# Scan layer: another order of its work on all four engines

## What is computed

```python
h = x @ fc1_w.T + fc1_b
xc, z = split(h @ in_proj_w.T)                     # 512 channels each
u = silu(causal_conv4(xc) + conv_b)
dt_low, Bm, Cm = split(u @ x_proj_w.T)             # 16, 16, 16
dt = softplus(dt_low @ dt_proj_w.T + dt_proj_b)
hstate = exp(dt * A) * hstate + (dt * u) * Bm      # per channel, 16 states, along 2048 steps
y = ((hstate * Cm).sum(states) + u * D) * silu(z)
s = (y @ out_proj_w.T) @ fc2_w.T + fc2_b
f = (silu(x @ w_gate.T) * (x @ w_up.T)) @ w_down.T # 768 hidden
```

## Time and profile before

| what | value |
|---|---|
| median of 3 runs | 2787.99 us (2785.57 to 2789.45) |
| profiled execution: its own time / span | 2788.2 us / 2786.4 us |
| first layer | up to about 859 us of the span |
| scan layer | about 859 to 2786 us |
| PE, DVE, ACT, POOL busy over the span | 91%, 84%, 72%, 72% |

### The profile page before, as it was taken

How to read it: one execution, slowest core, us unless ns; L and a number is a source line. 1 busy time by engine, 2 the same in 40 slices (tenths; PEclk the granted TensorE clock), 3 DMA queues, 4 the chain that set the end, 5 groups by cost and what they waited for, 6 DMA issues and landing times. The chain is left out here.

```text
span 2786.4 us, 37406 instructions
## 1 busy us (share of the span) xinstructions
PE 2542.0 (91%) x13454; PEld 1490.8 (54%) x13454; DVE 2333.8 (84%) x2899; ACT 2011.2 (72%) x3253; POOL 2013.2 (72%) x682
## 2 busy tenths in 40 slices
PE   7897899999976799999999999999999999999988
PEld 3454344443443465656656566565655656556565
DVE  7685777777733899898998989989899898998996
ACT  4222466666643798897988979889798897988974
POOL 0656011111211999999999999999999999999996
PEclk9898999999978799999999999999999999999999
DMA  6337999888541231321313213132131321313210
GB/s 188 116 116 179 260 218 236 205 200 224 211 161 49 105 130 29 117 92 46 130 26 119 92 46 130 25 120 92 46 130 24 121 92 46 130 24 114 92 46 8
DMA packets 121586, 316.00 MB, mean 113 GB/s; under 512 B 15517, under 2 KB 76445, under 8 KB 104878
## 3 DMA queue, kind: packets, MB, share of 16 engines
q1 hardware_dynamic: 91210, 233.32, 27.3%
q0 software_dynamic: 27888, 79.24, 10.3%
q10 hardware_dynamic: 2304, 1.05, 0.2%
HBM read 278.89 MB, written 43.13 MB: 116 GB/s over the span
## 5 line engine op out<-in xcount | busy, mean ns | idle before, releaser
L1523 DVE TENSOR_TENSOR_SCAN l_st<-l_p_a,l_hl,l_st 128x512 f32<-128x512 f32 x768 | 930.2, 1263 | 90.5 <-ACT l_p_a L1808 83.3
L1721 POOL TENSOR_TENSOR l_st<-l_st,lw_cs 128x2048 f32<-128x2048 f32 x192 | 878.4, 4634 | 3.2 <-ACT l_hl L1813 3.2
L1808 ACT ACTIVATE l_p_a<-l_dt,lw_a_neg 128x512 f32<-128x512 f32 x1024 | 666.5, 681 | 67.2 <-DVE keep_xg L1523 41.1
L1713 POOL TENSOR_TENSOR l_st<-l_bs,l_dtu 128x2048 f32<-128x2048 f32 (+1 forms) x128 | 555.1, 4337 | 57.2 <-PE l_p_y L2098 53.3
L2098 PEld LDWEIGHTS l_p_y<-keep_ident,l_st 128*128 128x128 f32 x3072 | 355.1, 145 | 118.6 <-issue 73.0
L2098 PE MATMUL l_p_y<-keep_ident,l_st 128*128 128x128 f32 x3072 | 380.5, 281 | 28.7 <-POOL l_st L1721 28.7
L1020 ACT ACTIVATE a_pr<-a_p_s 128x512 f32<-128x512 f32 x512 | 284.7, 596 | 143.8 <-PE a_p_s L1089 140.0
L931 DVE TENSOR_REDUCE a_mpart<-a_p_m 128x1 f32<-128x512 f32 x512 | 312.0, 679 | 12.2 <-PE a_p_m L1045 11.0
L1523 DVE TENSOR_TENSOR_SCAN keep_xg<-l_p_a,l_hl,keep_xg 128x512 f32<-128x512 f32 x256 | 314.5, 1265 | 1.6
L1721 POOL TENSOR_TENSOR keep_xg<-keep_xg,lw_cs 128x2048 f32<-128x2048 f32 x64 | 299.7, 4682 | 2.0 <-ACT l_hl L1813 2.0
L858 POOL DMA_DIRECT2D a_w<-in_w_dram x32 | 23.1, 737 | 327.2 <-PE a_p_m L1119 271.3
(11 more groups left out here) (246 smaller groups left out, 4007.9 us busy)
## 6 DMA issues: line engine op xcount, KB each, us to landing
l_bs<-s_bc SPq DMA_DIRECT2D x64, 1024.0 KB, 4.7
lw_cs<-s_bc SPq DMA_DIRECT2D x64, 1024.0 KB, 4.7
a_w<-in_w_dram POOLq DMA_DIRECT2D x32, 1024.0 KB, 12.0
late<-in_w_dram POOLq DMA_DIRECT2D x32, 1024.0 KB, 19.4
kx<-s_kp SPq DMA_DIRECT2D x96, 256.0 KB, 12.3
s_kp<-late SPq DMA_DIRECT2D x96, 128.0 KB, 2.1
s_vp<-late SPq DMA_DIRECT2D x16, 544.0 KB, 3.5
a_vg<-s_vp SPq DMA_DIRECT2D x16, 544.0 KB, 14.8
```

The costliest lines, as they stand in the source:

```text
L1523: eng.tensor_tensor_scan(st[k % NG][:, n, :], p_a[:, n, :], st[k % NG][:, n, :], hl[:, k, n:n + 1], ALU.mult, ALU.add).then_inc(scan_ok, 1)
L1713: eng.tensor_tensor(st[n][:, first:NG, :], bs[:, 4 * n + first:4 * n + 4, :], dtu[(k // NG) % 2][:, :].unsqueeze(1).broadcast_to([P, NG - ...
L1721: eng.tensor_tensor(st[n][:, :, :], st[n][:, :, :], cs[:, 4 * n:4 * n + 4, :], ALU.mult).then_inc(cm_ok, 1)
L1808: eng.activation(p_a[:, n, :], dt[c % 2][:, :], ACT.Exp, scale=a_neg[:, c, m:m + 1]).then_inc(dA_ok, 1)
```

## The change

It edits the scan layer alone. No product, no size and no instruction of the arithmetic is changed; the order on all four engines is, and so is the bank of many fills. The last up blocks (4 and 5), dt of block 1, the first half of the down product and the sums of slots 14 and 15 move on PE from the period after into the tile's own SCAN period. The transposition of the next tile's normed rows (`turn` 0) moves to the end of the period before it. DVE's input of slot 0 and `hidden(3)` move ahead of the last scan of the previous tile, and ACT's `normed` of the next tile and the fourth exponential of slot 0 move to the end of the period before.

```diff
+        FILLS = (("tr", 1, FRONT, 1), ("dn", 1, END, 0), ("yb", 3, END, 1), ("xc", 0, FRONT, 0), ("op", 0, END, 1),
+                 ("xc", 1, FRONT, 0), ("z", 0, SCAN, 1), ("dt", 2, SCAN, 0), ("z", 1, SCAN, 0), ("op", 1, END, 1),
+                 ("cv", 0, FRONT, 0), ("dt", 3, SCAN, 1), ("xc", 2, FRONT, 0), ("cv", 1, FRONT, 1), ("cv", 2, FRONT, 0),
+                 ("yb", 0, SCAN, 1), ("xc", 3, FRONT, 1), ("g", 0, SCAN, 0), ("g", 1, SCAN, 1), ("up", 0, SCAN, 1),
+                 ("cv", 3, FRONT, 0), ("up", 1, SCAN, 1), ("xd", 0, FRONT, 0), ("g", 2, SCAN, 1), ("yb", 1, SCAN, 0),
+                 ("z", 2, SCAN, 1), ("g", 3, SCAN, 0), ("up", 2, SCAN, 0), ("yb", 2, SCAN, 1), ("dt", 0, FRONT, 1),
+                 ("g", 4, SCAN, 0), ("z", 3, SCAN, 0), ("g", 5, SCAN, 1), ("up", 3, SCAN, 0), ("up", 4, SCAN, 1),
+                 ("up", 5, SCAN, 0), ("dt", 1, FRONT, 1), ("dn", 0, SCAN, 0), ("tr", 0, NEXT, 0))
...
 # DVE, first tile's convolution: waits for the last reader of its own bank
-                    wait(eng, done["cv"], c - 1)
+                    wait(eng, done["cv"], max([x + 1 for x in range(c) if bank("cv", x) == bank("cv", c)], default=0))
...
 # DVE, end of its period
+                    if front:
+                        step_size(q, 0)
+                    if scan:
                         scan_unit(s, 14, 3)
                         scan_unit(s, 15, 0)
-                        gated(s, o, 2)
                         scan_unit(s, 15, 1)
                         scan_unit(s, 15, 2)
+                    if front:
+                        dbu(q, 0)
+                    if scan:
+                        hidden(s, 3)
                         scan_unit(s, 15, 3)
...
 # POOL
                     if end:
+                        weighed(f, 11)
+                        weighed(f, 12)
                         dbu(f, 15)
+                        weighed(f, 13)
                     if scan:
                         step_input(s, o, 0)
...
                     if scan:
+                        weighed(s, 0)
                         step_input(s, o, 1)
-                        weighed(s, 0)
                         dbu(s, 3)
                         weighed(s, 1)
                         weighed(s, 2)
                         dbu(s, 5)
                         weighed(s, 3)
-                        step_input(s, o, 2)
-                    if end and f < NT - 1:
-                        residual(f)
-                    if scan:
                         weighed(s, 4)
                         dbu(s, 7)
                         weighed(s, 5)
+                        step_input(s, o, 2)
+                    if end:
+                        residual(f)
+                    if scan:
+                        dbu(s, 9)
                         weighed(s, 6)
-                        dbu(s, 9)
                         weighed(s, 7)
...
 # ACT, end of its period
+                        exp_unit(s, 15, 2)
                     if front:
                         step_input(q, 0)
                     if scan:
-                        exp_unit(s, 15, 2)
-                        exp_unit(s, 15, 3)
+                        gate_z(s, 3)
+                        gate_h(s, 5)
+                    if nxt:
+                        normed(q + 1)
+                    if scan:
+                        exp_tables()
+                        exp_unit(s, 15, 3)
                     if front:
                         exp_unit(q, 0, 0)
                         exp_unit(q, 0, 1)
-                    if scan:
-                        gate_z(s, 3)
-                    if front:
-                        exp_tables()
                         exp_unit(q, 0, 2)
+                        exp_unit(q, 0, 3)
```

More of the change, by code:

```diff
@@ L2050, in period @@
                         exp_unit(s, 14, 3)
+                        last(s, 13)
+                    if front:
+                        step_log(q, 0)
+                    if q == 0:
+                        norm_scale(1)
+                    if scan:
                         gate_h(s, 4)
[L2052 to L2055 removed]
                         exp_tables()
@@ L2228, in period @@
                     if end:
+                        back(q, f, p, 3)
+                    if front:
+                        conv_in(q, q, p, 0)
+                    if scan:
+                        sums(s, 1)
+                    if end:
                         mix(q, f, p, 0)
+                    if front:
+                        conv_in(q, q, p, 1)
                     if scan:
+                        gate_z(q, s, o, 0)
                         step_low(q, s, 2)
-                        sums(s, 1)
                         sums(s, 2)
+                        gate_z(q, s, o, 1)
+                        sums(s, 3)
                     if end:
```

336 lines of the change are left out of this document (144 added, 192 removed).

## The result

The changed kernel takes 2779.76 us (median; 2775.17 to 2782.18) where the kernel before takes 2786.89: a ratio of 0.9973, 95% interval 0.9963 to 0.9983. It is faster by 7.1 us; some 32 were forecast (2788.2 to 2756). The profiled execution took 2782.18 us, the slowest of the nine (span 2780.4; before 2788.2, span 2786.4).

What follows compares the result with a forecast made beforehand. POOL, 112.2 us busy plus 4.0 waiting per period, was taken as the bound. Gains of 25.5 (14 periods), 1.0 (last period), 2.0 (head) and 4.0 (end), 32.5 us, took 2788.2 to about 2756 us; range 2726 to 2797.

Steps and rivals of the forecast that it cites:

- likeliest case: The forecast of 2756 us with its inner bounds, 2740 to 2776 us, given a chance of 0.54.
- Rival (b): PE's sums 5, 7, 9, 11 each a us late: period 116.1 to 116.4, total 2780 to 2790 us; chance 0.13.
- the period: Steady scan-layer period: falls from 116.2 to 114.4 us, 1.8 each, 25.5 us over 14 periods.
- the end: After POOL's last product: dn0 done before it, 5.2 us gained, about 1.1 given back, 4 us net.
- signs of being wrong: Listed refutations: POOL wait over 1.5 us; slot 15's state-3 exponential over 9 us after `step_input` 0; DVE never idle at seam.
- the last period: Last scan period, without next tile and so without seam: shorter, 1.0 us gained.
- Predicted waits: POOL's waits, in us, before `weighed` 15, `weighed` 0, `dbu` 9, `dbu` 11 and `dbu` 13; added to 112.2 giving 114.55.
- more time in the middle: A longer seam gives PE more time mid-period, so 114.4 us was taken rather than the summed 114.55.
- Head: Start of the scan layer, first tile: `weighed` 0 about 2 us earlier, bounds 2 lost to 3 gained.
- Seam and tables: Tile's seam, from S (start of POOL's `step_input` 0): last exponential done at S + 8.4; added table loads cost ACT 2.6 us.
- (c): ACT's queue at the seam late: at 3.4 us late, 117.8 us a period, 2803 us; chance 0.21 with similar chains.
- (d): Table switch holds ACT another 1.28 us: 118.2 us a period, 2809 us; chance 0.02.

Runs made afterwards that it cites:

- e1: Changed kernel with ACT saving slot 4's ends straight behind the dt logarithm of block 2, ahead of three exponentials: 2776.86 us, 0.9966.
- e13: As e12_best, with dt product 1 of the next tile ahead of the sums of slot 14 on PE: 2769.2 us, 0.993.
- e16: As e13, with the edit of e1 added: 2764.82 us, 0.9912.
- e4_si0: Changed kernel with POOL's `step_input` 0 of the next tile ahead of `weighed` 13, as before the change: 2785.99 us, 0.9997.
- e9_seam: Changed kernel with the exponential of slot 15, state 3, ahead of ACT's copy, and up block 5 ahead of S14 on PE: 2774.55 us, 0.9945.
- e7_warm: Changed kernel with constant matrix products in the last scan period; at the end yb3 ahead of dn1, second output half in the other bank: 2774.24 us, 0.9946.
- e12_best: Edits of e9_seam and e7_warm, plus last tile's last scan ahead of `hidden` 3 and first tile's `conv_in` 3 ahead of `conv_out` 2: 2769.83 us, 0.9929.
- e3_tail: Changed kernel with op0 ahead of S1 in the last scan period; at the end yb3 ahead of dn1, second output half in the other bank: 2778.76 us, 0.9971.
- e17_dt2: As e13, with dt product 2 and the sums of slot 2 ahead of z0 on PE: 2774.06 us, 0.9948.
- e5_s9: Changed kernel with PE's sums of slot 9 ahead of the xd product instead of behind it: 2790.94 us, 1.0002.
- e10_undo_s1: Changed kernel with op0 ahead of S1 on PE again: 2797.91 us, 1.0034.
- e11_undo_s9: Changed kernel with g2 ahead of S9 on PE again: 2853.7 us, 1.0227.
- e2_exp15: Changed kernel with ACT's exponential of slot 15, state 3, ahead of the copy of dt*u, z3, g5 and the next tile's norm: 2773.78 us, 0.9957.
- e6_s7s9: Changed kernel with PE's S9 ahead of the xd product and S7 ahead of g1: 2796.57 us, 1.0031.

## Why the prediction was wrong

The direction was right, the amount was not: 32.5 us of gains were added up, 6.0 came in this execution. The median, 2779.76 us, lies in the wide range and outside the likeliest case, 2740 to 2776. Rival (b) all but names the time (2780 to 2790) but not the cause, since the period did shorten and the end was lost. One of the prediction's own signs of being wrong came: POOL waits over 1.5 us, 3.43 in the first period and 2.38, 1.51 and 1.57 in the last. Two steps failed by their mechanism and had the wrong sign, the last period and the end, 14.1 of the 26.5 us that are missing; the period, 8.1, was mis-sized.

**The period: mechanism right, size off.** Predicted waits 0.65, 0.4, 0.15, 0.65 and 0.5; measured 0.66, 0.34, 0, 0.35 and 0.53. One was missed: 0.70 before `weighed` 4, whose `last` now stands behind a logarithm and three exponentials. POOL's 112.3 and these five waits, 2.6, make the 114.9; the plain sum was 114.55. The further 0.15 for "more time in the middle" had no row and did not come. Over 14 periods 17.4 us instead of 25.5: 8.1 short, some 4.6 by the sum, 2.1 by the 0.15, and 1.4 because the gain of 1.8 was taken from 116.2, while the 14 periods were 116.12 each. The counting was of POOL's waits, which tells what a given order costs; what one of them is worth it does not tell (e1, e13, e16).

**The last period, 1.0 us forecast, 6.75 lost.** This step failed first. It was written down as one more, shorter period in one clause, with no walk. By the prediction's own rule, that only POOL's waits can be won, nothing could be gained: the kernel before has none there. Putting S1 ahead of op0 is right where PE has the front's blocks; without them PE idles 3.1 us ahead of S1, and in this execution its clock fell there, through a stretch in which POOL now hangs on it. Of POOL's 6.6 us of waits the clock accounts for some 3 (2.38 to 0.68 and 1.51 to 0, by e4_si0 and e9_seam), the seam for 1.1, the place of `hidden` 3 for 1.6, and 0.7 stand before `weighed` 4 in every period. The waits don't add up one by one: e7_warm took 2.38 + 1.51 us down to 0.69, but 0.91 before `dbu` 11 and 1.3 more before `weighed` 15 came up, and the period lost only 0.9. With the order of `hidden` 3 mended it is 107.6 (e12_best). e3_tail, with op0 ahead of S1 again and 114.2 us, shows that S1's move alone is not the cause.

**The end, 4.0 forecast, 2.35 lost.** The second step that failed: "Now dn0 is done before" took the place in the queue for a time. dn0 needs the last hidden block, which is up block 5, DVE, then PE: it starts 0.8 us before POOL ends, and S15, once ahead in time, is behind it. With the same-bank wait of the output halves mended, the end is 24.7 us (e3, e7), 0.6 under the time before; in e12_best, where POOL is done sooner, dn0 starts as POOL ends and the end is 25.3 again. The 4 us were not to be had in any run.

**Head, 2.0 forecast.** `weighed` 0 comes 2.85 us earlier against the first tile's shift (53.29 to 50.44); 1.27 of them only because `step_input` 1 now stands behind it, the rest is the mechanism named. By `weighed` 15 of tile 1 just 0.13 are left: that first period's waits behind `weighed` 0 are 3.43, 0.29 and 0.68 us (the first before the half `dbu` 9, for PE), where they were 0.98, 0.21 and 1.63. The clock is low in that period with either kernel (0.90, and 0.91 before). The first period was not walked either.

**Seam and tables: right.** The exponential starts at S + 7.7 as counted, rivals (c) and (d) did not come. A load is 1283 ns again, the silu starts 1.29 us after the load does, and ACT's busy time went from 98.4 to 101.3 us. By the Trainium skill, ScalarE: Activation LUTs, "What ACT_TABLE_LOAD costs", a switch takes some 1380 ns of drain more, by estimate 5.3 us for the added pair; the trace does not agree. There are 22 loads a period, as said; DVE's wait for the exponential is 1.65 us, under the 2 to 4 forecast.

In us, what was forecast less what came: 8.1 + 7.75 + 6.35 + 1.9, and 2.4 from the unchanged first layer, make the 26.5 that are missing.

## What to carry to other kernels

Walk the periods that lack a part (first, last, drain) as carefully as the steady one: an order that is right with other work in between can be wrong without it, and where an engine then idles, look at its clock too. A place in a queue is not a time; ask what the moved instruction itself waits for. In a loop whose engines are all over 85% busy, the waits of the fullest engine are where slack is paid out, not what closes the loop: follow the chain of waits, and before taking a wait away ask whether it is a link. A sum of waits is not a sum of gains, in the last period either. And before putting a change of time down to an order, compare the granted clock of the two stretches.

## What was not expected of the hardware

TensorE's granted clock fell behind one wait of 1.21 us in some periods of e17_dt2 and held in others, with the same instructions and waits; it cost 1.55 us each time. In e5_s9 it fell behind a wait of 1.83 us in every second period, at 1.9 us each time. Other waits left the period's clock at 1.00: the seam's of 1.13 us in e13_dt1 and e16_last4, and one of 1.33 us in e10_undo_s1. In the last scan period, behind the same 3.1 us of idle PE, the clock fell in three kernels (the one after, e1_last4, e11_undo_s9) and held in five (e2_exp15, e4_si0, e5_s9, e6_s7s9, e9_seam); with constant products as filler the wait was under 1 us and it held in all. Each is one profiled execution; what decides is not shown here.
